# Mixture-of-experts stage of a fused layer: the hidden units are split into two fp16 parts before they are transposed, the down product runs one tile later, the stage's head is reordered

## The reference

```python
x2d = hidden_states.reshape(T, D)                       # layernorm of x, T = 2048, D = 512
routing_weights = softmax(x2d @ gate_kernel)            # 32 experts
routing_weights, selected = top_k(routing_weights, 8)   # then divided by their sum
sorted_inputs = take(x2d, sort_idx // 8)                # 16384 rows, sorted by expert
w0 = ragged_dot(sorted_inputs, gate_proj, group_sizes)  # (512 -> 192) of the row's expert
w1 = ragged_dot(sorted_inputs, up_proj, group_sizes)
inter = silu(w0) * w1                                   # 192 hidden units
expert_out = ragged_dot(inter, down_proj, group_sizes)  # 192 -> 512
output = sum over the 8 experts of routing_weight * expert_out
```

## Time and profile before

| | us |
|---|---|
| median of three runs | 1480.61 |
| span of the profiled execution, first to last instruction | 1474.3 |
| PE busy in the span | 1382.7 |
| DVE, ACT, POOL busy | 1022.1, 505.4, 383.7 |
| expert stage: first gate and up product at 855.76, last add issued at 1466.42 | |

### The profile page before, as it was taken

How to read it: one execution, slowest core, us unless ns; L and a number is a source line. 1 busy time by engine, 2 the same in 40 slices (tenths; PEclk the granted TensorE clock), 3 DMA queues, 4 the chain that set the end, 5 groups by cost and what they waited for, 6 DMA issues and landing times.

```text
span 1474.3 us, 26984 instructions
## 1 busy us (share of the span) xinstructions
PE 1382.7 (94%) x7525; PEld 753.2 (51%) x7526; DVE 1022.1 (69%) x2467; ACT 505.4 (34%) x916; POOL 383.7 (26%) x313
## 2 busy tenths in 40 slices
PE   4799999999999999999999559999999999999997
PEld 3344444444444444455444236666666666666664
DVE  7879857976895656688776536666666666666664
ACT  1454543444435343422222113333333333333332
POOL 1000000000000000025556543444344344344443
PEclk9899999999999999999999769999999999999999
DMA  9975776766767778836748668889999888989785
GB/s 370 396 262 193 263 256 213 247 197 205 241 209 237 235 254 286 280 119 251 284 195 294 242 227 216 223 218 260 246 246 234 221 229 228 247 223 222 148 162 84
DMA packets 132696, 345.04 MB, mean 234 GB/s; under 512 B 15008, under 2 KB 19616, under 8 KB 125728
## 3 DMA queue, kind: packets, MB, share of 16 engines
q1 hardware_dynamic: 73488, 206.72, 41.6%
q0 software_dynamic: 34640, 85.74, 25.2%
q10 hardware_dynamic: 24512, 51.89, 10.8%
HBM read 192.68 MB, written 151.62 MB: 234 GB/s over the span
## 4 chain that ended last, share of the span: by engine, by line
PE 68%; DVE 16%; DMA 4%; issue 4%; ACT 3%; another core or an unknown queue 2%; ACTq 1%; SPq 1%; DVEq 0%; POOLq 0%
PE PS L1671 17%; PE PS L1673 17%; PE PS L1672 17%; PE PS L1933 5%; PE PS L1961 2%; PE PS L1962 2%; DMA split_experts<-HT 2%; DMA CST<-in_kv 1%; PE PS L1950 1%; DVE EX L1300 1%; PE PS L1951 1%; DVE EX L1306 1%; DVE nw L1027 1%; DMA X<-in_x 1%
## 5 line engine op out<-in xcount | busy, mean ns | idle before, releaser
L587 POOL DMA_INDIRECT out<-BIG,EX x159 | 247.2, 1555 | 354.9 <-issue 153.4
L1671 PE MATMUL PS<-BIG 128*128 (+1 forms) x795 | 269.5, 339 | 5.0 <-DVE BIG L1572 3.3
L1672 PE MATMUL PS<-BIG 128*128 (+1 forms) x795 | 269.5, 339 | 0.0
L1673 PE MATMUL PS<-BIG 128*128 (+1 forms) x795 | 269.5, 339 | 0.0
L1671 PE MATMUL PS<-HT,BIG 128*128 128x512 f16 (+1 forms) x512 | 194.1, 379 | 3.0 <-DVE HT L1101 1.4
L1672 PE MATMUL PS<-HT,BIG 128*128 128x512 f16 (+1 forms) x512 | 194.0, 379 | 0.0
L1673 PE MATMUL PS<-HT,BIG 128*128 128x512 f16 (+1 forms) x512 | 194.0, 379 | 0.0
L560 POOL DMA_INDIRECT rows_by_expert<-HT,POS x128 | 124.9, 976 | 122.6 <-DVE POS L1391 88.1
L1672 PE MATMUL PS<-BIG,EX 128*128 128x512 f16 (+1 forms) x376 | 143.8, 382 | 1.1 <-issue 1.1
L824 ACT ACTIVATE BIG<-PS 128x256 f16<-128x256 f32 x159 | 61.1, 384 | 243.3 <-PE PS L1951 229.0
L1673 PE MATMUL PS<-BIG,EX 128*128 128x512 f16 (+1 forms) x376 | 143.6, 382 | 0.4 <-issue 0.4
(11 more groups left out here) (264 smaller groups left out, 2218.0 us busy)
## 6 DMA issues: line engine op xcount, KB each, us to landing
BIG<-rows_by_expert ACTq DMA_DIRECT2D x159, 280.0 KB
HT<-in_experts SPq DMA_DIRECT2D x64, 640.0 KB, 4.6
BIG<-split_experts SPq DMA_DIRECT2D x32, 1152.0 KB
split_experts<-HT SPq DMA_DIRECT2D x96, 320.0 KB, 2.2
CST<-in_kv SPq DMA_DIRECT2D x64, 256.0 KB, 4.7
split_context<-RT SPq DMA_DIRECT2D x64, 256.0 KB, 4.5
BIG<-split_context SPq DMA_DIRECT2D x7, 2048.0 KB
rows_by_expert<-X SPq DMA_DIRECT2D x32, 280.0 KB
```

What stands on the lines that cost most here:

```text
L587: pool.indirect_dma_start(a_out, bass.IndirectOffsetOnAxis(ap=IDY[:, u % V:u % V + 1], axis=0), yt[u % V], None, compute_op=ALU.add).then_ ...
L1671: mm(out, lh, rh, start=first, stop=False)
L1672: mm(out, lh, rl, start=False, stop=False)
L1673: return mm(out, ll, rh, start=False, stop=last_group)
```

## The change

- **Order of split and transposition.** `hidden` makes 192 fp32 columns in one instruction; ACT writes their high part to `es` columns 0 to 191 (`hidden_hi`), DVE the low part of the last 64 units to columns 192 to 255 and that of the first 128 to columns 256 to 383 (`hidden_lo`). PE transposes the three fp16 blocks into one bank read as fp16 (`hidden_transpose`), and ACT copies 384 columns to SBUF (`hidden_copy`). The middle block then holds the high parts of 64 units above their low parts, and is multiplied by a doubled high block and by a doubled low block of the down weights. The number of down matmuls stays 5.
- **Weights.** Both copies of the 64 rows get a full low part: `E16 = 2 * EW` = 5120 columns, a second-half low store of 1280 columns in place of 768, no L1123.
- **Pipeline.** PE per tile: transposition of t+3, gate and up of t+2, hidden transposition of t+1, down of t. `LEAD = 7`.
- **Tables.** The row table and the table of waits are made first and signalled by a first raise of `s_tab`, for which ACT waits; the others wait for the second. Their entries are shifted by one (`LATE = 1`), so that the loads still start on sixteen bytes. `load_counts` copies each loaded count through a register instruction that clamps it from below.
- **Head.** ACT runs silu and splits of the first tiles between the early loads. POOL scatters five columns of tile 13 before it waits for tile 14. SP writes 8 pads ahead of the loop and stays 8 ahead.

```diff
-EL = KC * GU + D
-E16 = EW + EL
+E16 = 2 * EW
-LEAD = 6
+LEAD = 7
+LATE = 1
+def load_counts(eng, name, table, least, most):
+    loaded = [eng.alloc_register(f"{name}{i}") for i in range(table.shape[-1])]
+    held = [eng.alloc_register(f"{name}_held{i}") for i in range(table.shape[-1])]
+    eng.reg_load(loaded, table)
+    for to, of in zip(held, loaded):
+        eng.reg_alu(to, of, least, ALU.max)
+        eng.free_register(of)
+    return [eng.snap(x, donate=True, min_val=least, max_val=most) for x in held]
...
-            for e in range(WP):
+            for e in range(2 * WP):
                 pad_expert(e, 16 * e)
-            sp.wait_ge(s_tab, 1)
+            sp.wait_ge(s_tab, 2)
...
-            for t in range(NT - 3, NT):
+            scatter_rows(NT - 3, range(5))
+            for t in range(NT - 2, NT):
                 scatter_rows(t, range(4))
...
             def hidden_hi(t, p):
+                act.wait_ge(s_ea, t + 1)
+                act.activation(es[p][:, 0:M], ea[p], ACT.Copy).then_inc(s_ah2, 1)
+
+            def hidden_copy(t, p):
                 act.wait_ge(s_at, t + 1)
-                act.activation(eah[p], PS[:, 4, 0:2 * P], ACT.Copy).then_inc(s_ah2, 1)
+                act.activation(eT[p], hT, ACT.Copy).then_inc(s_ac, 1)
...
+            for t in range(1, 4):
+                load_early(t)
+            tile_silu(0, 0)
             tile_hi(1, 1, due[1])
-            tile_silu(0, 0)
+            load_early(4)
+            hidden_hi(0, 0)
+            tile_hi(2, 0, due[2])
+            load_early(5)
+            tile_silu(1, 1)
+            hidden_copy(0, 0)
+            hidden_hi(1, 1)
+            load_early(6)
             with act.Fori(0, LOOPS) as it:
-                rows, due = rows_at("tile_row", it * U + 4, U + 4), experts_due("tile_due", it * U, U + 8)
+                rows, due = rows_at("tile_row", it * U + LEAD, U), experts_due("tile_due", it * U + 3, U + LEAD - 3)
                 for u in range(U):
                     t = it * U + u
-
-                    hidden_hi(t, u % 2)
-                    tile_hi(t + 2, u % 2, due[u + 2])
+                    tile_hi(t + 3, (u + 3) % 2, due[u])
                     if u < TOPK - LEAD:
                         act.wait_ge(s_add[LEAD + u], LANDED)
-                    load_tile((u + LEAD) % U, t + (V + LEAD - U + 1), rows[u + LEAD - 4], due[u + LEAD])
-                    tile_silu(t + 1, (u + 1) % 2)
+                    load_tile((u + LEAD) % U, t + (V + LEAD - U + 1), rows[u], due[u + LEAD - 3])
+                    tile_silu(t + 2, u % 2)
+                    hidden_copy(t + 1, (u + 1) % 2)
+                    hidden_hi(t + 2, u % 2)
...
+            def hidden(t, p):
+                dve.wait_ge(s_es, t + 1)
+                v.scalar_tensor_tensor(ea[p], PS[:, 2 + p, M:2 * M], 1.0 / (H_S * E_S), eg[p], ALU.mult, ALU.mult).then_inc(s_ea, 1)
+
             def hidden_lo(t, p):
                 dve.wait_ge(s_ah2, t + 1)
-                v.tensor_tensor(eal[p], PS[:, 4, 0:2 * P], eah[p], ALU.subtract).then_inc(s_al2, 1)
+                v.tensor_tensor(es[p][:, M:2 * P], ea[p][:, P:M], es[p][:, P:M], ALU.subtract)
+                v.tensor_tensor(es[p][:, 2 * P:3 * P], ea[p][:, 0:P], es[p][:, 0:P], ALU.subtract).then_inc(s_al2, 1)
...
                     t = it * U + u
-                    hidden_lo(t, u % 2)
-                    tile_lo(t + 2, u % 2)
-                    hidden(t + 1, (u + 1) % 2)
+                    tile_lo(t + 3, (u + 3) % 2)
+                    hidden(t + 2, u % 2)
+                    hidden_lo(t + 2, u % 2)
                     weigh(t, u, it * (U // V) + u // V, experts[u])
...
+            def hidden_transpose(t, p):
+                if not isinstance(t, int) or t:
+                    pe.wait_ge(s_ac, t)
+                pe.wait_ge(s_al2, t + 1)
+                for k in range(3):
+                    last = nc.tensor.transpose(hT[:, k * P:(k + 1) * P], es[p][:, k * P:(k + 1) * P], ident16)
+                last.then_inc(s_at, 1)
...
             tile_transpose(0, 0, 0)
             pe.wait_ge(s_wl, 16)
-            pe.wait_ge(s_xl, 1)
             tile_up(0, 0, 0)
             tile_transpose(1, 1, 0)
-            pe.wait_ge(s_tab, 1)
+            tile_transpose(2, 2, 0)
+            pe.wait_ge(s_tab, 2)
+            at = weights_at("first_weights", 0, 4)
+            tile_up(1, 1, at[1])
+            hidden_transpose(0, 0)
             with pe.Fori(0, LOOPS) as it:
                 at = weights_at("tile_weights", it * U, U + 4)
                 for u in range(U):
                     t = it * U + u
-                    tile_transpose(t + 2, (u + 2) % U, it + (u + 2) // U)
-                    pe.wait_ge(s_ea, t + 1)
-                    hidden_transpose(u % 2)
-                    tile_up(t + 1, (u + 1) % 2, at[u + 1])
+                    tile_transpose(t + 3, (u + 3) % U, it + (u + 3) // U)
+                    tile_up(t + 2, u % 2, at[u + 2])
+                    hidden_transpose(t + 1, (u + 1) % 2)
                     tile_down(t, u % 2, at[u])
```

More of the change, by code:

```diff
@@ L263, in build @@
         o += 2 * M
-        ea = [BIG[:, o + i * 2 * P:o + (i + 1) * 2 * P] for i in range(2)]
-        o += 4 * P
-        eah = [f16(BIG, o + i * P, (2 * P,)) for i in range(2)]
-        eal = [f16(BIG, o + (2 + i) * P, (2 * P,)) for i in range(2)]
+        ea = [BIG[:, o + i * M:o + (i + 1) * M] for i in range(2)]
+        o += 2 * M
+        es = [f16(BIG, o + i * M, (2 * M,)) for i in range(2)]
+        o += 2 * M
+        eT = [f16(BIG, o + i * 192, (3 * P,)) for i in range(2)]
         o = [0]
@@ L571, in _ @@
                 scatter_rows(t)
-            for t in range(NT - 3, NT):
+            scatter_rows(NT - 3, range(5))
+            for t in range(NT - 2, NT):
                 scatter_rows(t, range(4))
             for w in range(4, TOPK):
-                for t in range(NT - 3, NT):
+                for t in range(NT - 3 + (w == 4), NT):
                     scatter_rows(t, (w,))
-            pool.wait_ge(s_tab, 1)
+            pool.wait_ge(s_tab, 2)
             pool.wait_ge(s_res, 16 * B)
@@ L844, in _ @@
             act.wait_ge(s_tab, 1)
-            rows, due = rows_at("first_row", 0, U), experts_due("first_due", 0, U)
+            first = [act.alloc_register(f"first{i}") for i in range(2 * U)]
+            act.reg_load(first[0:U], TROWS[0:1, 0:U])
+            act.reg_load(first[U:], TAB[0:1, 1, 0:U])
+            rows = [act.snap(x, donate=True, min_val=0, max_val=NE * CAP + (SPARES - 1) * P) for x in first[LATE:U]]
+            due = [act.alloc_register(f"first_due{i}") for i in range(U - LATE)]
@@ L846, in _, with load_early @@
+            for to, of in zip(due, first[U + LATE:]):
+                act.reg_alu(to, of, 16, ALU.max)
+            for of in [first[0]] + first[U:]:
+                act.free_register(of)
+            due = [act.snap(x, donate=True, min_val=16, max_val=16 * NE) for x in due]
             act.wait_ge(s_spare, 16)
-            for t in range(1, LEAD):
+            def load_early(t):
                 act.wait_ge(s_add[t], LANDED)
                 load_tile(t, 0, rows[t], due[t])
+            for t in range(1, 4):
+                load_early(t)
@@ L1530, in _ @@
             v.tensor_copy(CH[0:NE, 0:1], CI[0:NE, 1:2]).then_inc(s_tq, 1)
+            v.tensor_scalar(CH[0:NE, 2:3], CI[0:NE, 1:2], -1.0, float(LIST), ALU.mult, ALU.add).then_inc(s_tq, 1)
             dve.wait_ge(s_tp, 2)
@@ L1533, in _ @@
             v.tensor_copy(CH[0:NE, 1:2], PS[0:NE, 1, 0:1]).then_inc(s_tq, 1)
-            dve.wait_ge(s_tq, 4)
+            dve.wait_ge(s_tq, 5)
             v.tensor_scalar(TCMP[0:NE, :], TROW[0:NE, :], CE[0:NE, 0:1], None, ALU.is_ge).then_inc(s_tq, 1)
             dve.wait_ge(s_tp, 3)
-            erow, start = PS[0:1, 2, 0:TABLE], PS[0:1, 2, TABLE:2 * TABLE]
+            place, erow, start = PS[0:1, 6, 0:TABLE], PS[0:1, 2, 0:TABLE], PS[0:1, 2, TABLE:2 * TABLE]
             trow = TROW[0:1, :]
+            v.tensor_tensor(TWK[:, 1, :], place, trow, ALU.add).then_inc(s_tq, 1)
@@ L1553, in _ @@
[L1553 removed]
+            dve.wait_ge(s_tq, 19)
             v.tensor_tensor(TAB[:, 4, :], TWK[:, 3, :], start, ALU.add).then_inc(s_tq, 1)
[L1555 to L1558 removed]
@@ L1589, in _ @@
             tile_lo(0, 0)
+            hidden(0, 0)
             tile_lo(1, 1)
-            hidden(0, 0)
+            hidden_lo(0, 0)
+            tile_lo(2, 0)
+            hidden(1, 1)
+            hidden_lo(1, 1)
             with dve.Fori(0, LOOPS) as it:
```

138 lines of the change are left out of this document (65 added, 73 removed).

## The result

| | before | after |
|---|---|---|
| median of the runs | 1480.53 us (4) | 1462.43 us (4: 1460.85, 1461.27, 1463.59, 1464.08) |
| ratio, 95% interval | | 0.9883 [0.9871, 0.9896] |
| span of the profiled execution | 1474.3 us | 1461.8 us |
| routing ends (last router row written by VectorE) | 844.90 | 846.12 |
| product of tile 0 / of tile 1 starts | 855.76 / 872.23 | 856.51 / 870.32 |

1463.5 us was predicted, 1462.4 measured, 18.1 us less than before. The two profiled executions lie only 12.5 us apart. After the change a run's time is 1.8 to 1.9 us above its span in all four runs; by that the profiled execution of before was a short one, 1474.3 + 1.8 = 1476.1, 4.5 us under its median. The "6.3 us around the span" of the prediction are thus 1.8 around it and 4.5 of spread.

A forecast was written before the change was run, and what follows sets the result against it. TensorE's own stream, 94% busy, was taken as the bound. Terms -9.0 - 1 - 8 + 0.5 - 1.5 + 2.6 - 0.6 gave -17; 1474.3 - 17 + 6.3 = 1463.6, say 1463.5 us, range 1455 to 1470.

The forecast's parts named there:

- The "6.3 us around the span": Whole run: the median of the runs lies 6.3 us above the profiled span of 1474.3, added back to the forecast.
- transpositions: Hidden units on TensorE: three fp16 transpositions at 0.054 us replace two fp32 ones; -9.0 us, bounds -22 and +17.
- stalls in the stage: Expert stage: down a tile later removes about half of TensorE's 2.2 us of split waits; -1 us, bounds 0 and -2.2.
- head up to the product of tile 1, register load: Head of the expert stage: silu and split of tile 1 before loads 4 to 6, -8 us; TensorE register load +0.5.
- clock: Half clock behind the head: less idle time ahead of it gives -1.5 us, bounds 0 and -2.9.
- weights, split; other engines in a tile: Larger weight split on VectorE and shifted ACT and VectorE work per tile: 0; outer case 0.1 us a tile (16 us).
- adds hold TensorE: Expert stage: more weight bytes lengthen each landing by about 0.4 us, and a faster stream meets the adds; +2.6 us.
- from the last up product on: Tail: three down products in place of two run behind the last up product and cover the copy; -0.6 us.
- the head's gain is lost: Rival, head: ACT's hold falls on silu or split of tile 1; 6.5 of 8 us go, 1470 us; chance 0.12.
- the adds hold TensorE: Rival, expert stage: the adds hold the stream, leaving a small gain, 1469 to 1480 us; chance 0.14.
- the prediction's sign of being wrong, over 5 us of such waits: Expert stage: the forecast is wrong if VectorE waits for adds for more than 5 us in all.
- the two chains differ by 1%: Expert stage: adds span 507.3 us and VectorE's weighting 513.2 us; given as support for the rival that adds hold TensorE.

The follow-up runs named there:

- experiment 6: The kernel before with its loaded wait counts held at 16 or more by one register operation each; 1481.88 us, ratio 1.0012.
- experiment 4: The changed kernel with each tile's three fp16 transpositions of the hidden units done twice; ratio 1.0065, all six executions 1458.1 to 1461.2 us.
- experiment 1: The changed kernel, but POOL's last nine scatters (columns 5 to 7) wait until tile 1 is split; ratio 0.9927.
- experiment 3: The changed kernel with four pads ahead of the loop in place of 8, as before; ratio 0.9883, shorter executions 1432.4 to 1433.9 us.
- experiment 8: The changed kernel with a POOL memset before every fourth add's issue; two executions at 1464.9 and 1467.6 us, four at 1496.5 to 1512.8.
- experiment 7: The kernel of experiment 6 with silu of tile 0 and the split of tile 1 ahead of loads 4 and 5 on ACT; 1481.89 us, ratio 1.0012.
- experiment 10: The changed kernel, unedited, on the second kind of chip; ratio 0.9924, three of seven executions at 1432.3 to 1433.0 us.
- experiment 5: The changed kernel, unedited, on the first kind of chip; ratio 0.9884, five shorter executions 1462.1 to 1465.9 us.
- the first job: The job of the result itself: the kernel before at 1480.53 us and the changed kernel at 1462.43 us.
- The pause in the scatters: The kernel of experiment 1, run in two jobs, both on the second kind of chip; ratios 0.9927 and 0.9923.
- experiment 12: The kernel of experiment 3 again, beside the changed kernel; ratio 0.9874, three shortest of seven 1431.6 to 1433.6 us.
- experiment 11: The changed kernel, but the 28 later experts' weights load 4096 of 5120 columns; ratio 0.9879, all four executions 1431.0 to 1435.3 us.
- experiment 2: The changed kernel with ACT's order in the head as before (loads 1 to 5 first); ratio 0.9931, six of twelve executions 1436.3 to 1438.1 us.

## Why the prediction was right, and where it was not

*The sum, on the two profiled executions (term, forecast, measured):*

| term | forecast | measured |
|---|---|---|
| transpositions | -9.0 | -8.1: (3.685 - 3.633) x 157 |
| stalls in the stage | -1 | -4.0: from the ninth tile on TensorE's tiles exceed the steady length by 5.7 us in all before, 1.7 after |
| head up to the product of tile 1, register load | -7.5 | -1.9 |
| clock | -1.5 | about 0 |
| weights, split; other engines in a tile | 0 | not seen: TensorE is busy 158.41 of 160 us in the FFN stage, and the undisturbed tile is as long as its stream |
| adds hold TensorE | +2.6 | 0 in these executions |
| from the last up product on | -0.6 | +2.5, of it 1.1 us a down product that was moved there out of the stretch before |

The measured terms add up as -1.9 up to 870.32; then 588.44 (872.23 to 1460.67) to 575.31 (870.32 to 1445.63) = -13.1 us to the last up product (-8.1, -4.0, -1.1 for the moved down product, 0.1 over); then 13.63 to 16.17 = +2.5; together -12.5. The sum forecast -17 for these two executions, so it was 4.5 us too hopeful. The medians differ by 18.1, since the profiled execution of before lies 4.5 us under its median and that of after (1461.8 + 1.8) 1.1 over its. What one execution of the kernel before loses against another is seen in experiment 6, whose kernel is all but the same and whose trace is 4.4 us longer: its routing ends 1.9 us later, and it takes 1.9 us more from the product of tile 1 to the last up product (its stalls from the ninth tile on are 9.2 us in place of 5.7). So the largest term, TensorE's stream, was right in mechanism and size. That the time came within 1.1 us was luck: the other terms failed in opposite directions, and the base was off by as much as their sum.

*Transpositions: right.* The rate by column of the prediction gives 0.054 us, experiment 4 gives 0.056, and the undisturbed tile fell by 0.052 us where 0.057 was forecast.

*Stalls: right in kind, too small.* The forecast halved 2.2 us of waits that the profile credits to the split. The lengths of the tiles show 5.7 us lost in six turns. Some 3.3 us of it stand in front of the down product. Some 2.1 stand in front of the first transposition of a turn, where TensorE's own table load came late, a wait that the prediction did not look at (first its loads, ns min/median/max; then its row in the view of waits, total, times, longest):

```profile
L104 PEldq TENSOR_LOAD <-EX x20: 844/887/2239, 857.5 to 1438.6; - x20
```

```profile
PE PS L1933 <- issue: 1.5, 3, 0.5
```

The view of waits counts from a matmul's modelled end, which lies behind the next start in a stream, and so both its rows are smaller than what the tiles lose. After the change only 1.7 is left (0.8, 0.4 and 0.8 us in the traces of experiments 1, 3 and 8; 9.2 and 9.0 in those of 6 and 7 with the old pipeline), beyond the bound of -2.2 that I gave. No run parts the later down product from the other changes of the pipeline. The lengths of the tiles, not the list of waits, were the row to size it by.

*Head: this step failed.* It said: "Silu needs the product of tile 0, whose last matmul runs as the transpositions start, so 859.8", and took the order on ACT to be worth 8 us. Silu ran at 864.54 and the split of tile 1 at 868.86, and the product of tile 1 only 1.9 us earlier than before. The 1.9 us lie behind the hold: from the split of tile 1 to the product of tile 1 it is 868.94 to 872.23 = 3.3 us before and 868.86 to 870.32 = 1.5 after, because table load, silu and the transposition of the hidden units no longer stand between. Of the signs, the product of tile 1 did not start at 861 to 864, and ACT was idle from 860 to 869, though not without a semaphore: it waited for one that was late. The rival "the head's gain is lost" had the place and the time (870 to 871; 870.32), but not the reason: it made the 3.65 us of the earlier trace rows ACT's own instruction supply. Four things stand against that. The semaphore records under experiments 6 and 7 show the signals themselves late, and ACT starting 0.02 us behind them. The queues that moved data from 848 to 872 us (changed kernel: packets, MB, share) are those of POOL, SP and ACT alone, none for instructions:

```profile
q0 software_dynamic: 1204, 4.31, 45.5%
q1 hardware_dynamic: 809, 1.63, 20.4%
q10 hardware_dynamic: 719, 1.43, 19.8%
```

The same program on the other kind of chip has no hold (experiment 10). In experiments 5 to 8 the hold of the split ends 3.7 to 4.4 us behind POOL's last scatter, in the first job 4.1 and 3.6, whatever ACT has in front; experiment 7 moved silu ahead of two loads and bought nothing. The Trainium skill, page "Runtime: NRT & Kernel Launch", section "Instruction fetch mechanics", which the rival drew on, thus does not account for it. What makes the signals late is not shown: on one kind of chip they come late while POOL's scatters run, on the other at once at the same GB/s. The last of the three signals is counted 3.6 to 4.3 us behind the last scatter's issue and 6.7 to 7.7 us behind the end of the transposition that it reports; both distances are steady, so these traces do not single out the scatters. In the changed kernel's trace the signal for silu came at 864.52, before the last scatter was issued. The pause in the scatters was built to test that; both times it ran on the chip without the hold, and it stays open.

On the other kind of chip the step is right in mechanism, with 4 to 5 us for 8: order restored, product of tile 1 10.3 us behind that of tile 0 in place of 5.4, 1436.3 to 1438.1 in place of 1432.3 to 1433.0. The 8 us came from a trace in which most of ACT's idle time was the hold.

*Clock: nothing.* The idle time in front of the product of tile 1 stayed (8.9 us; before, 10.5 in front of the transposition just ahead of it), and so did the half clock behind it: matmuls of 384 columns stand 0.32 us apart (1.2 GHz) up to 876.5, against 0.16 behind. In experiment 10, with 1.1 us of idle time in front of it, that product runs at 0.16 from its start.

*Adds: right to watch, wrong in form.* The forecast added a constant to every landing. Landings did not grow: the mean step between experts went from 9.70 to 9.35 us, though the DMA engines are busier. What exists instead is a matter of phase, seen in experiments 3 and 12: the step behind an add that lands beside a weight load takes some 3 us more, the chain of adds falls behind, and can meet the next load in the same way. That this is what throws an execution out of step is argued from the traces, not tested. As long as the chain is in time, nothing is held; once it is out, 10 us of the stage go (experiment 12), and in the traces of experiments 10 and 5 (executions of 1461.7 and 1494.3 us, one on each kind of chip) VectorE waits 43.2 us for adds in 15 places and 49.8 us in 18. So the prediction's sign of being wrong, over 5 us of such waits, is absent in the trace of the result and present in these. The kernel before and experiment 4, with 3.68 and 3.80 us a tile, show no such loss: all 78 executions of before and of experiments 6 and 7 lie within 1% of each other on one kind of chip, and the six of experiment 4 within 0.3%. That fits the prediction's "the two chains differ by 1%"; the skill's rule that all queues share the 16 engines (the Trainium skill, page "DMA: Bandwidth & Descriptors", section "Issuing engines are not separate DMA queues") agrees with 12.4 against 6.7 us for the same step. The higher load's part is small: experiment 11, with 5.6% less, moved the steps within their spread. What starts it in one execution and not in the next is not shown. The rival "the adds hold TensorE" had 0.14 for what happens in part of the executions.

*Tail: wrong sign.* Of the +2.5 us, 0.6 lie between the starts of the last up product and of the last down product, 1.1 between that and the last add's issue (the last two tiles are weighted 1.1 us apart, and two adds on POOL are 1.86 us apart: 1451.23, 1453.09), 0.8 behind it. One more down product runs there, and the forecast looked at TensorE alone.

## What to carry to other kernels

A stretch of idle time is only worth what its releaser says: where the profile names none ("remote", "unknown queue"), an earlier order may buy nothing, and the term's range has to start at zero. Size stalls by the lengths of the repeated unit, not by the list of waits. Where a chain of transfers runs beside the bound with 1% to spare, a faster bound need not cost a little each time: here the kernel fell out of step in some executions and lost nothing in the others, so look at single executions, not at the median alone.

## What the runs showed of the hardware

- One fp16 transposition of 128 columns costs TensorE 0.056 us at full clock (experiment 4), a fp32 one 0.11.
- Silu's table load does not wait for silu's operand: after the change it runs at 856.22 to 857.50 and silu at 864.54; in experiment 2, where a split stands in front, it costs its 1.28 us behind it.
- The same program took 1480.5 us on one kind of chip and 1451 on the other. Between the changed kernel's trace and that of experiment 3, 31.3 us apart, 22.0 are there by the product of tile 0 (856.51 and 834.52), 8.3 more by the product of tile 1 (13.8 and 5.5 us behind it), 1.0 behind that. What makes the 22 us is not looked into here.
- On the first kind of chip TensorE's signals in the head were counted 4.6 to 9.3 us behind the end of the work that they report (six traces; that end is modelled, from a measured start); on the second, within 0.02 us of it (experiment 10).
- The landing of an accumulating indirect write of 128 rows varies: the same step to the next expert took 6.7 us with 1.3 MB of weights issued 4.9 us behind the add and 12.4 us with the weights issued beside it (experiments 3 and 12). In the latter the add landed after 10.5 us.
